# The second half's expert routing started in the shared experts, 4-bit codes decoded by two word shifts, and norm and latents moved forward, in a two-layer transformer kernel on one Trainium2 core

## What is computed

```
x  = L0_attn_x                                  # [8, 256, 256]
xn = layernorm(x)
x  = x + L0_attn(xn) + L0_ffn(xn)
xn = layernorm(x)
x  = x + L1_attn(xn) + L1_ffn(xn)
# L0_attn: vhat = q * cumsum(k * v), times Wo
# L0_ffn : shared experts (352 wide) + top 2 of 8 experts (176 wide), weighted
#   scores = sigmoid(xn @ gate_w.T); topk_w, topk_idx = top_k(scores, 2)
#   topk_w = topk_w / (topk_w.sum() + 1e-20) * 2.5
# L1_attn: latent attention, 16 heads, causal softmax; the latents (85 and 128 wide) are
#   layer-normed themselves
# L1_ffn : weights stored as 4-bit codes with a scale for every 32:
#   low = W & 15; high = W >> 4 & 15; vals = LUT[idx] * scales
#   out = (gelu(xt @ Wg.T) * (xt @ Wu.T)) @ Wd.T     # 2048 wide
```

## Time and profile before

| | |
|---|---|
| median of 3 runs | 780.81 us (777.93 to 781.98) |
| the profiled execution | 781.96 us, span 780.1 us |
| busy in the span | PE 678.9 us (87%), DVE 523.9 (67%), ACT 390.6 (50%), POOL 355.2 (46%) |
| mean granted TensorE clock | 0.975 of full speed |
| shared stage | about 0 to 132 us |
| expert stage | about 132 to 281 us |
| second layer | about 281 to 780 us, four groups |

### The profile page before, as it was taken

The page is one execution under the profiler, slowest core; times in us unless marked ns, Lnnn a source line. Parts: engine busy times, 40 slices in busy tenths (PEclk is TensorE's granted clock), DMA queues, the critical chain, the costliest instruction groups (busy, mean ns, idle before and its releaser), DMA issues.

```text
span 780.1 us, 13300 instructions
## 1 busy us (share of the span) xinstructions
PE 678.9 (87%) x4656; PEld 543.7 (70%) x4656; DVE 523.9 (67%) x1004; ACT 390.6 (50%) x679; POOL 355.2 (46%) x299
## 2 busy tenths in 40 slices
PE   5897898894959879799989989989988998999996
PEld 4675677784848667577667767767866777777774
DVE  6885855884886746567485858486768668467745
ACT  3644423442543644274575455385448276447263
POOL 1416276376576226145163527164616353416353
PEclk9999899897998999999999999999999999999999
DMA  8427735766885274512003303002402000201100
GB/s 313 130 94 223 267 121 179 224 202 221 294 277 181 77 279 116 179 25 58 2 2 108 82 2 82 2 1 69 121 2 65 19 1 28 62 23 44 39 2 28
DMA packets 66804, 82.76 MB, mean 106 GB/s; under 512 B 7090, under 2 KB 50354, under 8 KB 66738
## 3 DMA queue, kind: packets, MB, share of 16 engines
q1 hardware_dynamic: 63156, 73.39, 29.7%
q0 software_dynamic: 3072, 8.39, 3.3%
q10 hardware_dynamic: 512, 0.13, 0.1%
HBM read 40.34 MB, written 28.84 MB: 89 GB/s over the span
## 4 chain that ended last, share of the span: by engine, by line
PE 37%; ACT 9%; DVE 9%; issue 5%; DMA 2%; POOL 2%; ACTq 1%; POOLq 0%; DVEq 0%
PE acc L632 4%; PE acc L634 3%; PE acc L633 3%; PE pv L632 2%; PE pm L632 2%; PE pm L634 2%; PE pm L633 2%; PE pv L634 2%; PE pv L633 2%; PE ring L955 2%; PE ring L985 2%; DVE hf L2067 2%; DVE mx L2151 2%; ACT act L1428 1%; PE ring L957 1%
## 5 line engine op out<-in xcount | busy, mean ns | idle before, releaser
L1531 POOL TENSOR_TENSOR hl<-hf,hh 128x512 fp32r<-128x512 f32 (+1 forms) x76 | 99.3, 1307 | 231.5 <-ACT hh L1235 231.4
L1235 ACT ACTIVATE hh<-hf 128x512 fp32r<-128x512 f32 (+1 forms) x76 | 47.7, 629 | 85.5 <-DVE hf L2067 69.8
L632 PE MATMUL acc<-hh,wh 128*128 128x512 f32 (+1 forms) x168 | 70.6, 420 | 7.6 <-POOL hl L1531 7.6
L2067 DVE TENSOR_TENSOR hf<-hf,pv 128x512 f32<-128x512 f32 x64 | 43.6, 682 | 39.7 <-PE pv L634 38.6
L2151 DVE TENSOR_REDUCE mx<-ring 128x2 f32<-128x512 f32 (+1 forms) x96 | 61.7, 684 | 11.5 <-PE ring L957 11.3
L633 PE MATMUL acc<-hh,wl 128*128 128x512 f32 (+1 forms) x168 | 66.3, 395 | 0.0
L634 PE MATMUL acc<-hl,wh 128*128 128x512 f32 (+1 forms) x168 | 66.3, 395 | 0.0
L1410 ACT ACTIVATE hf<-pm 128x512 f32<-128x512 f32 x56 | 33.3, 595 | 58.6 <-PE pm L634 55.5
L1672 POOL TENSOR_TENSOR pl<-act,ph 128x512 f16<-128x512 f32 x32 | 41.7, 1303 | 39.9 <-ACT ph L1433 37.0
L632 PE MATMUL pv<-xh,wh 128*128 128x512 f32 x128 | 54.0, 422 | 1.5 <-DVE hf L2067 1.5
L632 PE MATMUL pm<-xh,wh 128*128 128x512 f32 x112 | 48.9, 437 | 2.9 <-issue 2.9
(11 more groups left out here) (289 smaller groups left out, 2117.6 us busy)
## 6 DMA issues: line engine op xcount, KB each, us to landing
w4s<-w4hl SPq DMA_DIRECT2D x16, 512.0 KB, 3.8
ws<-qs SPq DMA_DIRECT2D x12, 512.0 KB, 5.1
qT<-qp SPq DMA_DIRECT2D x96, 64.0 KB, 2.6
kT<-kp SPq DMA_DIRECT2D x96, 64.0 KB, 2.7
xs<-yg SPq DMA_DIRECT2D x2, 2944.0 KB, 12.5
late<-xs SPq DMA_DIRECT2D x22, 256.0 KB, 3.1
ys<-act SPq DMA_DIRECT2D x22, 256.0 KB, 3.4
stage<-w SPq DMA_DIRECT2D x8, 608.0 KB, 4.5
```

The source lines that it names most:

```text
L632: pe.matmul(o, w_hi, x_hi, start=first, stop=False, skip_group_check=True)
L1235: a.activation(h_parts(n)[0][0:rows, :], hf[0:rows, n % 2, :], ACT.Copy).then_inc(s_hh, 1)
L1531: return pool.tensor_tensor(dst, src, hi.bitcast(F32), ALU.subtract)
L2067: v.tensor_tensor(hf[:, n % 2, :], hf[:, n % 2, :], pv[:, :], ALU.mult).then_inc(s_h, 1)
```

## The change

- The second half's logits are turned and its sigmoid taken at the end of the shared stage. `choose(1, ...)` runs around the first `rows_lo`, then `shares`, `offsets`, `positions` and `owners` at steps 0 to 3, where they were at 1, 2, 3, 5, 6 and 7. `rows_out_to(1, ...)` is spread between units 4 to 7 on POOL. The first half's `offsets` and `positions` go behind the first `gated` of group 2, and `residual(1)` goes between the two `choose`.
- A unit's codes are decoded by two instructions on 32-bit words instead of three on 16-bit ones: a left shift that puts the 4 bits at the top, then an arithmetic right shift by 19 with a mask. The odd unit is decoded in place in `ws`, the even one into `even`. POOL reads the low half of each word, every second fp16. The units stand at steps 3, 5, ..., 41.
- The first of a token's two expert rows is weighted on ACT (`weigh_first`), the second is still multiplied and added on DVE.
- `back`, `add_rows` and the layernorm steps move up by one step. `rows_back(0)` and `rows_back(1)` come one unit earlier, and `rows_back` 4 to 6 move from the second layer into the loop; 7 comes one place earlier in group 0.
- `latents(0)` comes right behind the last `expert_in`. Their norm is made in the loop's tail, between the last two `expert_rows`. The last pair's result goes to `xn`, so that it doesn't wait for a store, and `gate1(0)` waits for one `expert_rows` less.
- SP issues the small constants one per step, and waits for the stores ahead of the rows of ones.

The diff, cut to its core (8 spaces of indent are taken off):

```diff
-W4_AT = dict(zip((0, 2, 4, 6, 8, 10, 13, 16, 18, 20, 22, 24, 26, 28, 30, 32, 34, 36, 38, 41), range(4, 2 * NQ)))
+W4_AT = {3 + 2 * i: 4 + i for i in range(2 * NQ - 4)}
...
-mag = sb("mag", [P, QW], U16, c0)
-sign = sb("sign", [P, QW], U16, c0)
-code = sb("code", [P, 2, QW], U16, c0)
+even = sb("even", [P, 2, QW], I32, c0)
...
 def back_rows(c):
     apart = lambda t: t[:, c % 2, :].rearrange("p (b d) -> p b d", d=D)
-    if c < 4:
+    if c < 7:
         return (yg[:, :, :], ex[:, 0, :].rearrange("p (b d) -> p b d", d=D),
-                ex[:, 1, :].rearrange("p (b d) -> p b d", d=D), xn[:, 0:2, :])[c]
+                ex[:, 1, :].rearrange("p (b d) -> p b d", d=D), xn[:, 0:2, :])[c % 4]
+    if c == 7:
+        return apart(act)
     return apart(act if c % 4 < 2 else ex)
...
+def rows_from(pp):
+    if pp == HALVES * PAIRS - 1:
+        return xn[:, 2:2 + pair_tiles(pp), :]
+    b = 2 * (pp % 2)
+    return rows_out[:, b:b + pair_tiles(pp), :]
...
-            sp.wait_ge(s_bits, 4 * (p - 1))
+            sp.wait_ge(s_bits, 2 * (p - 1))
             sp.wait_ge(s_w4, 4 * (p - 1))
...
+    for done in s_yd:
+        sp.wait_ge(done, 16 * PAIRS)
     sp.dma_start(kT[SLOT:SLOT + 2, :, :], ones_rows.bitcast(BF16)).then_inc(s_ones, 16)
...
+        if q == 2:
+            pe.wait_ge(s_rt, ROUTE_STEPS + 25)
...
-        if g == 1:
-            turn_logits(0)
+        if g % HG == 1:
+            turn_logits(g // HG)
...
+        if q == HALVES * TILES - 1:
+            for i in range(2):
+                pe.wait_ge(s_wlo[i], len(lo_of[i]))
+            normed(G)
+            latents(0)
...
-        if q == 0:
-            turn_logits(1)
-        if q == 5:
+        if q == 1:
             counts(1)
         if q == TILES + 9:
             back(0)
             back(1)
-        if q == TILES + 12:
+        if q == TILES + 11:
             back(2)
             back(3)
-        if q == TILES + 14:
+        if q == TILES + 13:
             ln_mean(G)
-        if q == TILES + 16:
+        if q == TILES + 15:
             ln_var(G)
         if q >= 2:
             expert_out(q - 2, at[q - 2])
     turn_gated(HALVES * TILES - 1)
-    for i in range(2):
-        pe.wait_ge(s_wlo[i], len(lo_of[i]))
-    normed(G)
-    latents(0)
...
-                pe.wait_ge(s_yo, HALVES * PAIRS)
+                pe.wait_ge(s_yo, HALVES * PAIRS - 1)
...
+            if g == 0 and t == 0:
+                pe.wait_ge(s_yo, HALVES * PAIRS)
             half1(g, t, 1).then_inc(s_gu, 1)
...
+    def weigh_first(c):
+        h, i = c // TT, c % TT
+        first = back_rows(c)[:, 0, :]
+        a.wait_ge(s_gat[c % 4], 32 * (c // 4 + 1))
+        if c == 0:
+            a.wait_ge(s_rt, ROUTE_STEPS * HALVES)
+        a.activation(first, first, ACT.Copy, scale=share[:, h, 0, i:i + 1]).then_inc(s_cw0, 1)
...
-        if pp >= 2:
+        if 2 <= pp < HALVES * PAIRS - 1:
             a.wait_ge(s_yd[pp % 2], 16 * (pp // 2))
         bank = (pm, pv)[pp % 2][:, 0:n * D].rearrange("p (t d) -> p t d", t=n)
-        a.activation(rows_out[:, 2 * (pp % 2):2 * (pp % 2) + n, :], bank, ACT.Copy).then_inc(s_yo, 1)
+        a.activation(rows_from(pp), bank, ACT.Copy).then_inc(s_yo, 1)
...
+        if g == G - 1:
+            scores_of(1)
...
-        if q == 0:
-            scores_of(1)
         if W4_AT.get(q, 1) % 2 == 0:
             scales_hi(W4_AT[q] // 2)
         if q == TILES + 2:
             weights(13)
         if q == TILES + 4:
             weights(14)
-        if q == TILES + 15:
+        if 7 <= q - TILES < 11:
+            weigh_first(q - TILES - 7)
+        if q == TILES + 14:
             ln_square(G)
-        if q == TILES + 17:
+        if q == TILES + 16:
             ln_std(G)
-        if q == TILES + 20:
+        if q == TILES + 19:
             ln_hi(G)
         if q >= 2 and pair_done(q - 2) is not None:
             expert_rows(pair_done(q - 2))
     gated_hi(HALVES * TILES - 1)
-    expert_rows(HALVES * PAIRS - 2)
-    expert_rows(HALVES * PAIRS - 1)
-
-    for done in s_yd:
-        a.wait_ge(done, 16 * PAIRS)
-
     def latents_std(nb):
         a.wait_ge(s_bn, 8 * (nb + 1))
         a.activation(cstd[:, :], mv[:, :, 1], ACT.Sqrt, bias=epsb[:, :]).then_inc(s_cstd, 1)
+
+    expert_rows(HALVES * PAIRS - 2)
+    latents_std(0)
+    expert_rows(HALVES * PAIRS - 1)
...
+        if g < G - 1:
+            weigh_first(4 * g + 4)
         gelu(3)
         hi(3)
+        if g < G - 1:
+            weigh_first(4 * g + 5)
...
+        if g < G - 1:
+            weigh_first(4 * g + 6)
         hi(4)
+        if g < G - 1:
+            weigh_first(4 * g + 7)
...
-        w = code[:, k % 2, :].bitcast(F16)
+        w = codes_of(k).bitcast(F16).rearrange("p (n h) -> p n h", h=2)[:, :, 0]
...
-        if c in (0, 4):
+        if c in (0, 7):
...
+    split_h(11, ST_M[2])
     w4_parts(2)
-    split_h(11, ST_M[2])
     w4_parts(3)
     for k in range(4, 8):
+        rows_out_to(1, 2 * k - 8, 2 * k - 7)
         w4_parts(k)
-    rows_out_to(1, 0, 1, 2)
-    w4_parts(8)
-    rows_out_to(1, 3, 4, 5)
-    w4_parts(9)
-    rows_out_to(1, 6, 7)
-    for k in range(10, 17):
+    for k in range(8, 16):
         w4_parts(k)
     rows_back(0)
     rows_back(1)
+    w4_parts(16)
+    rows_back(2)
+    rows_back(3)
     w4_parts(17)
-    rows_back(2)
+    weights(13)
     w4_parts(18)
-    rows_back(3)
-    weights(13)
-    for k in range(19, 2 * NQ):
+    w4_parts(19)
+    for k in range(20, 23):
+        rows_back(k - 16)
         w4_parts(k)
+    w4_parts(23)
...
-        v.wait_ge(s_gat[c % 4], 32 * (c // 4 + 1))
-        v.tensor_scalar(rows[:, 0, :], rows[:, 0, :], share[:, h, 0, i:i + 1], None, ALU.mult).then_inc(s_cw, 1)
-        v.wait_ge(s_cw, 2 * c + 1)
+        v.wait_ge(s_cw0, c + 1)
...
-        if k:
-            v.wait_ge(s_code, k)
-        low16 = words(n).bitcast(U16).rearrange("p (n h) -> p n h", h=2)[:, :, 0]
-        v.tensor_scalar(mag[:, :], low16, 9 - 4 * j, 7 << 9, ALU.logical_shift_left,
-                        ALU.bitwise_and).then_inc(s_bits, 1)
-        v.tensor_scalar(sign[:, :], low16, 12 - 4 * j, 1 << 15, ALU.logical_shift_left,
-                        ALU.bitwise_and).then_inc(s_bits, 1)
+        if j:
+            v.wait_ge(s_bits, k)
+        elif k >= 4:
+            v.wait_ge(s_w4, 2 * (k - 3))
+        v.tensor_scalar(codes_of(k), words(n), 28 - 4 * j, None, ALU.logical_shift_left).then_inc(s_bits, 1)
...
-        v.wait_ge(s_bits, 2 * k + 2)
-        if k >= 2:
-            v.wait_ge(s_w4, 2 * (k - 1))
-        v.tensor_tensor(code[:, j, :], mag[:, :], sign[:, :], ALU.bitwise_or).then_inc(s_code, 1)
+        v.wait_ge(s_bits, k + 1)
+        v.tensor_scalar(codes_of(k), codes_of(k), 19, 1 << 15 | 7 << 9, ALU.arith_shift_right,
+                        ALU.bitwise_and).then_inc(s_code, 1)
...
-        if g == 2:
-            offsets(0)
-            positions(0)
-            owners(0)
-        if g == 3:
-            codes(2)
...
+                residual(1)
                 choose(0, 1)
                 shares(0)
+            if g == 2 and t == 0:
+                offsets(0)
+                positions(0)
             if g == 2 and t == 1:
+                owners(0)
                 codes(0)
             if g == 2 and t == 2:
                 codes(1)
-            if g == 3 and t == 1:
+            if g == 3 and t == 0:
+                codes(2)
+            if g == 3 and t == 2:
                 codes(3)
-        if g < G - 1:
+        if g in (0, 2):
...
+    choose(1, 0)
     rows_lo(0)
+    choose(1, 1)
     residual(G - 1)
     for q in range(HALVES * TILES):
         expert_gated(q)
         if turned_in(q) is not None:
             rows_lo(turned_in(q))
+        if q == HALVES * TILES - 1:
+            bias_latents(0)
         if q >= 1:
             gated_lo(q - 1)
+        if q == 0:
+            shares(1)
         if q == 1:
-            choose(1, 0)
+            offsets(1)
         if q == 2:
-            choose(1, 1)
+            positions(1)
         if q == 3:
-            shares(1)
-        if q == 5:
-            offsets(1)
-        if q == 6:
-            positions(1)
-        if q == 7:
             owners(1)
         if q - 1 in W4_AT:
             code_join(W4_AT[q - 1])
             turn_weights()
         if q == TILES + 4:
             weights(14)
-        if q - TILES in (7, 8, 10, 11):
-            weigh_rows((7, 8, 10, 11).index(q - TILES))
+        if 7 <= q - TILES < 11:
+            weigh_rows(q - TILES - 7)
         if q == TILES + 10:
             add_rows(0)
             add_rows(1)
-        if q == TILES + 13:
+        if q == TILES + 12:
             add_rows(2)
             add_rows(3)
-        if q == TILES + 15:
+        if q == TILES + 14:
             ln_centre(G)
+        if q == TILES + 16:
+            ln_inverse(G, 0, 1)
         if q == TILES + 17:
-            ln_inverse(G, 0, 1)
+            ln_inverse(G, 2, 3)
         if q == TILES + 18:
-            ln_inverse(G, 2, 3)
```

(5 more changed lines are left out.)

115 lines of the change are left out of this document (56 added, 59 removed).

## The result

The changed kernel takes 769.27 us (median of 4 runs, 768.64 to 769.39), the kernel before 781.35 us (median of 4 runs, 777.93 to 781.98). The ratio is 0.986, with a 95% interval of 0.983 to 0.989. That is 12 us less, where 28 were forecast; 769 lies above the range of 742 to 767. One execution of the variant with three edits took 927 us at a granted clock of 0.66, where its others show 0.98 to 0.99; such executions are left out of every figure here.

A forecast was written before the change was run, and what follows sets the result against it. No engine is full over the expert stage: it is a ring of PE, ACT, DVE with two big holes and a slow beginning. Eight terms sum to -28.0 from 781.96, giving 753.96, median 752.8 (say 753); range 742 to 767.

The forecast's parts named there:

- A: Shared stage: PE's idle at 78.76 goes, but ACT's wait for codes and later first-half positions offset it; 0 us (-2 to +2).
- C: First hole, PE's 12.84 us step: earlier positions let POOL end sooner, some 3.5 us of wait remain; -7 us (-11 to -1).
- E: Second hole, near step 32: first weighting goes to ACT, returned rows are fetched a unit sooner; -6 us (-8 to -3).
- H: Second layer: earlier fetches of returned rows and shorter DVE chains in three groups; -3 us (-5 to -1).
- D: Steps 19 to 32: two-instruction word decode saves DVE 0.41 us a unit, less joins held by POOL; -2 us (-5 to +1).
- Rival 1: The first hole only moves: unit 7 and codes late, hole returns at step 15; 761 us, chance 0.2.
- B: First steps of the expert loop: two table loads leave the ring, `choose` fits DVE's idle; -3.5 us (-6 to -1).
- F: Steps 33 to 45: five units at -0.41 us each, three more fetches fit POOL's idle; -2 us (-5 to +1).
- G: Seam between expert stage and second layer: table load and root come earlier, the store wait goes; -4.5 us (-6 to -3).
- Rival 2: Word decode on DVE is slow, 0.68 us each, and both instructions held by POOL; 760 us, chance 0.08.
- Rival 3: Holes are worth more than their length, as PE's clock stays up behind them; -34 to -45 us, chance 0.08.
- Rival 4: Slower than before: POOL reads every second fp16 badly, products at 2.48 us; +6.5, 787 us, chance 0.04.

The follow-up runs named there:

- the variant with three edits: Changed kernel with scatter spread among the units, GpSimd waiting for the weighting ahead of unit 17, and for both choices at the loop's start: 763.35 us.
- both places of the wait: GpSimd waits until four returned tiles are weighted: ahead of unit 17 in the changed kernel, 768.47 us; behind it, 763.75, or 758.74 with scatter spread.
- the wait alone: Changed kernel plus one GpSimd wait behind unit 17, until the four returned tiles are weighted; scatter as in the changed kernel: 763.75 us, ratio 0.980.
- the wait for the choice: Changed kernel plus a GpSimd wait ahead of units 2 and 3, until both choices of the second half are made: 768.91 us, ratio 0.986.
- the spread scatter: Changed kernel with the second half's scatter spread among units 4 to 10, not two tiles ahead of each of units 4 to 7: 766.13 us, ratio 0.981.
- the route back in the loop: Changed kernel with the second half's route back in the expert loop (choices at steps 1 and 2, shares at 3, offsets, positions, owners at 5 to 7): 774.78 us.
- the kernel with both edits: Changed kernel with the scatter spread among the units and GpSimd's wait for the weighting behind unit 17: 758.74 us, ratio 0.973.
- the order alone: Changed kernel with the seam's order undone (norm, first latents, deviation late again), the other buffer and dropped store waits kept: 770.82 us, ratio 0.987.
- the best kernels: Changed kernel with scatter spread and wait behind unit 17, 758.74 us; weighting also one step later, 757.56; waits for each choice on top, 757.24.

## Why the prediction was wrong, step by step

The direction was right, the size was off by 16 us. Of the eight terms A, C and E carry most of the difference, 17 us together; H gives 3.4 back.

**The second hole (E), the largest miss.** The step was "I leave 1 for the returned rows 2 and 3, which POOL now fetches in one run", and ahead of it that the wait for the returned rows was the cause. It named the 3.14 us at 226.61 as part of this hole, moved that multiplication to ScalarE, and didn't ask again what had made it so long. It was an instruction held by GpSimd, and the change put a longer run of GpSimd (units 17 and 18 with piece 13 between them) right beside the next such instruction. The prediction itself called this row a held one behind term D, for the joins, and left the hold out of the term where it decided. That GpSimd's run is the cause is shown by both places of the wait (0.48, 1.33 and 2.04 us in place of 6.13), and that this made the hole by the 5.5 us that the wait alone gives back.

**The first hole (C).** The step was "`positions(1)` ends near 141", and from it that "some 3.5 us remain" at step 15. The scatter started at 146.34, so unit 7 ended at 177.06 instead of 171, and the codes landed at 181.13. With the loop started on time, by the wait for the choice, it was 143.63: half of the miss is the late start, and the other half is that the small steps, some of them held, take longer than the three steps of the loop that they were given. Rival 1 said just this: a hole of 8 us by `codes_in(5)`, though at step 18 and not 15. It had a chance of 0.2, and its time of 761 had no room for E. Shown by the spread scatter, which removes this hole alone, and from the other side by the route back in the loop, with which the load goes out 4.6 us later.

**The shared stage (A).** A priced the move of `residual(1)` and the scatter, and the step that failed stands in B: "`choose` fits where DVE idles before the loop". It put `choose(1, 0)` ahead of `rows_lo(0)` at nothing. With 3.2 us of hold and 1.1 of lateness A was +4.3. Yet curing the hold gave nothing: in the first 17 steps other instructions were held instead. How much of the lead each of them took is not worked out. So A's miss and B's small excess belong together: 0.2 us for both, where -3.5 was forecast.

**The rest of the ring (D and F).** D measured -3.5 for -2, F +1.3 for -2. The old decode in the changed kernel took the same time (31.7 us for D's stretch and 35.4 for F's, against 31.0 and 33.4), so it isn't the new decode that made most of D, nor that made F slower. The prediction took 1532 ns a unit; it is (795 + 598 + 500 + 417) / 2 = 1155 ns for the two instructions. The term was mis-sized on the good side; by the run with the old decode it is worth 0.8 us in D's stretch, and nothing in the time. What made F slower is open. It follows the second hole, and in the kernel with both edits and in that with the wait alone the same ten steps take 32.3 us instead of 33.4.

**The seam (G)** was right in size, -4.3 for -4.5. Its working let the gelu come 4.3 sooner by the root ahead of the last copy, and named the store's wait only beside it. By the order alone it is 1.3; the rest is the buffer and the waits.

**The second layer (H)** was mis-sized: -6.4 for -3, all of it between the first gelu and the first residual. The tile that waited for returned rows is the place. ScalarE's activation behind it in the kernel before, and the one that answers to it after:

```profile
322.71 0.60 ACT L1410 ACTIVATE hf<-pm 128x512 f32<-128x512 f32 x1 [5.91 <-PE pm L634]
```

```profile
311.09 0.60 ACT L1430 ACTIVATE hf<-pm 128x512 f32<-128x512 f32 x1 [1.40 <-PE pm L645]
```

The activations ahead of these start at 311.77 and 304.90, so this one tile is 4.75 us shorter. I had priced PE's 3.38 us at 1.8. The 0.7 us a group for VectorE's chain, which I counted three times, did not appear: from the first residual to the second it is 123.0 us before and 122.8 after.

**The rivals.** Rival 2 (the words are slow): the shift and the masked shift take 0.41 us when free, not 0.68; but that the words are held is true: one took 2.75 us in the changed kernel, and 5.13 with the scatter spread and the wait. Its argument, "the two-source one kept to 414", was no evidence: in the trace of before that instruction never started during a run of GpSimd, as it stands where GpSimd mostly waits for its result; in the changed kernel with the old decode it did so once, and took 2.40. Rival 3 (the holes are worth more than their length) had no trial in the changed kernel, where both stayed; its sum was off as well, since -34 is 747 and not 742. Rival 4 (GpSimd reads every second fp16 badly): its products take 1.14 to 1.46 us, mean 1.23 for 1.25 before. It does not exist. Rival 5 (the queues crowd): codes land in 6.0 us instead of 5.1, but the best kernels move the same bytes, so it is not what bounds.
